# A recurrent transformer layer on one core: where local attention mixes, copies and shifts its values

## The reference, cut to what matters

```
q, k, v = split(xn @ w_qkv.T); q, k = rotary(q), rotary(k)
bq = windows(q)                      # 8 windows of 64
bk, bv = look_around(windows(k)), look_around(windows(v))   # previous window + own
attn = softmax(mask(bq @ bk.T / 8))
out = (attn @ bv) ... @ w_lo.T
```

## Time and profile before

| | us |
|---|---|
| median of 3 executions | 759.84 |
| lowest and highest | 759.74, 760.39 |
| profiled execution, its span | 759.2 |
| PE busy | 719.5 |
| DVE busy | 474.4 |
| ACT busy | 424.8 |
| POOL busy | 234.5 |

### The profile page before, as it was taken

One profiled execution on the slowest core, in us unless ns is written; L12 is line 12 of the kernel. 1 busy time (PEld: TensorE's weight loads), 2 busy tenths in 40 slices (PEclk: granted clock), 3 DMA queues, 4 the chain that ended last, 5 costly groups with the idle time before them and its releaser, 6 DMA issues.

```text
span 759.2 us, 17502 instructions
## 1 busy us (share of the span) xinstructions
PE 719.5 (95%) x6154; PEld 572.1 (75%) x6160; DVE 474.4 (62%) x1021; ACT 424.8 (56%) x1548; POOL 234.5 (31%) x364
## 2 busy tenths in 40 slices
PE   4899999999999899999999999989999999999996
PEld 3678888878887577777777778868788787877866
DVE  6433333359886787787877786574655646556575
ACT  2444444432223567677677677684756647557473
POOL 2130000000003598777766673023223131331000
PEclk9999999999999999999999999999999999999999
DMA  8701000000000323333333332000000000000001
GB/s 246 302 1 57 1 0 0 0 0 0 0 1 15 94 68 78 88 75 92 78 85 79 81 92 53 2 2 18 10 7 17 0 19 1 2 0 0 0 1 55
DMA packets 26190, 32.70 MB, mean 43 GB/s; under 512 B 7184, under 2 KB 15888, under 8 KB 25488
## 3 DMA queue, kind: packets, MB, share of 16 engines
q1 hardware_dynamic: 24848, 29.27, 14.0%
q0 software_dynamic: 1280, 2.62, 1.3%
HBM read 12.98 MB, written 2.10 MB: 20 GB/s over the span
## 4 chain that ended last, share of the span: by engine, by line
PE 55%; issue 10%; POOL 9%; DVE 8%; POOLq 7%; ACT 6%; DMA 2%; DVEq 1%; SPq 1%; ACTq 0%
PE ps L778 9%; PE ps L766 9%; PE ps L1034 7%; PE ps L1101 6%; POOLq L587 5%; PE ps L1068 4%; PE ps L1084 4%; POOL early L579 4%; PE ps L753 4%; PE ps L747 4%; PE ps L1077 2%; ACT stage L1343 2%; POOL stage L586 2%; POOLq L589 2%; POOL early L598 2%
## 5 line engine op out<-in xcount | busy, mean ns | idle before, releaser
L579 POOL TENSOR_TENSOR early<-stage 128x512 f32<-128x512 f32 x64 | 89.9, 1425 | 54.9 <-DVE stage L1708 39.7
L1343 ACT ACTIVATE stage<-ps,nmB 128x128 f32<-128x128 f32 x256 | 90.2, 381 | 27.1 <-DVE nmB L1741 26.9
L1412 ACT ACTIVATE early<-ps,nmC 128x128 f32<-128x128 f32 (+1 forms) x224 | 78.0, 370 | 30.9 <-DVE nmC L1802 30.9
L778 PE MATMUL ps<-stage 128*128 128x128 f32 (+2 forms) x448 | 86.1, 321 | 1.4 <-DVE stage L1602 1.3
L766 PE MATMUL ps<-stage,early 128*128 128x128 f32 (+2 forms) x448 | 87.1, 324 | 0.0
L766 PEld LDWEIGHTS ps<-stage,early 128*128 128x128 f32 x448 | 66.0, 194 | 24.5 <-issue 15.5
L778 PEld LDWEIGHTS ps<-stage 128*128 128x128 f32 x448 | 65.5, 191 | 12.1 <-issue 1.9
L1068 PEld LDWEIGHTS ps<-stage,early 128*128 128x128 f32 x448 | 55.5, 191 | 22.3 <-issue 22.1
L1288 ACT ACTIVATE stage<-ps 128x512 f32<-128x512 f32 x64 | 31.5, 491 | 65.2 <-PE ps L766 65.2
L1597 DVE COPY stage<-ps 128x512 f32<-128x512 f32 x32 | 22.1, 692 | 71.3 <-PE ps L753 70.9
L1799 DVE TENSOR_REDUCE nmC<-ps 128x4 f32<-128x512 f32 (+1 forms) x56 | 36.5, 652 | 46.6 <-PE ps L1068 46.6
(11 more groups left out here) (203 smaller groups left out, 1516.2 us busy)
## 6 DMA issues: line engine op xcount, KB each, us to landing
early<-early SPq DMA_DIRECT2D x256, 64.0 KB, 2.0
x<-in_x SPq DMA_DIRECT2D x4, 256.0 KB, 3.7
stage<-in_cq SPq DMA_DIRECT2D x1, 1024.0 KB, 8.1
stage<-in_ck SPq DMA_DIRECT2D x1, 1024.0 KB, 10.1
stage<-in_cv SPq DMA_DIRECT2D x1, 1024.0 KB, 12.1
stage<-in_co SPq DMA_DIRECT2D x1, 1024.0 KB, 14.1
early<-in_wqk SPq DMA_DIRECT2D x1, 1024.0 KB, 16.0
xrows<-xhat SPq DMA_DIRECT2D x1, 1024.0 KB, 5.6
```

What stands on the lines that cost most here:

```text
L579: pool.tensor_tensor(to, a, b, (ALU.subtract, ALU.add)[f]).then_inc(rot_in, 1)
L778: t = pe.matmul(ps[:, b, q0:q1], vN[:, b % 2, m, :], simA[:, b % 2, s, at:at + q1 - q0], start=False, stop=False, skip_group_check=True)
L1343: t = act.activation(pB[:, u % 2, at, :], ps[:, 4 + h, i * P:(i + 1) * P], ACT.Exp, bias=nmB[:, u % 2, at:at + 1], accum_out=rsB[:, u % 2, ...
L1412: act.activation(pC[:, k, hg, 0:n], ps[:, 5 + k, hg * P:hg * P + n], ACT.Exp, bias=nmC[:, k, hg:hg + 1], accum_out=rsC[:, k, hg:hg + 1])
```

## The change: what it does

It moves work between the rounds of three loops. DVE and SP keep theirs.

- PE, round u: **mix(u-2)**, scores(u), turn(u-1), **project(u+4)**, out(u-2), **values(u)**. Mix moves from the middle of round u+1 to directly in front of the masks and scores of round u+2; values move from the round before to the end of their own.
- ACT, round u: **mixed(u-2)**, probs(u-1), exp(u, 0), exp(u, 1), **valued(u)**.
- POOL, round u: **shifted(u-1)**, add(u+4), extra(u). Before it was shifted(u+1): the shift moves two rounds back in POOL's order. The shift of unit 0 ahead of the loop is gone, that of unit 31 stands behind it.
- The mix, its copy and the output product of unit 30 now stand in the first steps of the next stage.

```diff
 # POOL
-            shifted(0)
             add(2)
             add(3)
...
             for u in range(NU):
-                if u + 1 < NU:
-                    shifted(u + 1)
+                if u > 0:
+                    shifted(u - 1)
                 if u + 4 < NU:
                     add(u + 4)
...
+            shifted(NU - 1)
 # PE, b_values(u) and b_turn_probs(u)
-                if u >= 2:
-                    pe.wait_ge(pT_in, 2 * (u - 1))
+                if u >= 1:
+                    pe.wait_ge(pT_in, 2 * u - 1)
...
-                pe.wait_ge(vB_in, min(u + 2, NU))
+                pe.wait_ge(vB_in, u + 1)
 # PE, ahead of the loop and in it
-            b_values(0)
...
             for u in range(NU):
+                if u > 1:
+                    b_mix(u - 2)
                 b_scores(u)
                 if u > 0:
                     b_turn_probs(u - 1)
-                if u > 1:
-                    b_out(u - 2)
-                if u > 0:
-                    b_mix(u - 1)
-                if u + 1 < NU:
-                    b_values(u + 1)
                 if u + 4 < NU:
                     b_project(u + 4)
...
+                if u > 1:
+                    b_out(u - 2)
+                b_values(u)
 # PE, start of the next stage
                 if not before:
+                    b_mix(end - 1)
                     b_turn_probs(end)
-                    b_out(end - 1)
...
                 expand(g, b, it, 0)
+                if not before:
+                    b_out(end - 1)
 # ACT
-            b_valued(0)
...
             for u in range(NU):
+                if u > 1:
+                    b_mixed(u - 2)
                 if u > 0:
                     b_probs(u - 1)
                 b_exp(u, 0)
                 b_exp(u, 1)
-                if u > 0:
-                    b_mixed(u - 1)
-                if u + 1 < NU:
-                    b_valued(u + 1)
+                b_valued(u)
```

More of the change, by code:

```diff
@@ L1439, in sequence @@
                 if not before:
+                    b_mixed(end - 1)
                     b_probs(end)
```

## The result

The changed kernel takes 802.72 us (801.58 to 805.45, five runs) against 759.74 us (759.28 to 760.39): a ratio of 1.058, 95% interval 1.0561 to 1.0599, slower. The forecast was 792 with a range of 780 to 808. In the profiled execution the span went from 759.2 to 799.8 us, +40.6.

A forecast was written before the change was run, and what follows sets the result against it. PE and POOL were taken as both nearly full; the late shift closes a two-round loop, adding 32.0 us (239.4 against 207.4 to scores(29)), other edits -1.05 and +1.1, to the median 759.84: 792 us, range 780 to 808.

The forecast's parts named there:

- a loop over two rounds: Local attention: scores(v), exponentials, norm, rope, add(v+4), extra, shifted(v), mix(v), scores(v+2); 16.79 us with a gather, against 14.3 before.
- gather and shift 3.94: POOL, rounds with a gather: 0.16 to start, 0.99 gather, 0.62 first copy, 1.66 drain, 0.51 second copy; 3.94 us.
- 3.13: POOL's add when normalizing runs beside it, in us; the prediction charged 2.50 instead, saying 3.13 would make the sum 8.8 higher.
- the fallen clock: Rival: PE's granted clock falls from 2.4 to 1.2 GHz, a round is 14.1 us of PE, about 985 us; 3%.
- The sum: Local attention: scores(29) 239.4 us behind scores(0) against 207.4, +32.0; the even chain puts scores(28) 231.7 behind.
- values(0) off the path ahead: Ahead of the loop, values(0) and its copy leave the path where PE goes straight on: -1.05 us.
- The end: values(31) come to stand in round 31, ahead of mix(30) and the last turn: +1.1 us.
- The rest at nothing: Other edits, such as dropped mix waits, earlier project(u+4), turn(u) needing valued(u), and later out(30): no effect on time.
- The first: Rival: the shift stays hidden and POOL's own pace goes on binding, needing a loop of at most 14.3 us; 758.8 us, 7%.
- the drain behind each gather: POOL, between shift copies: 1.66 us charged each; a rival had it shrink to 0.13, giving 777 us, 7%.
- All contended: Rival: adds at 3.13, normalizing at 1.51 and drains at 2.4 us together, +27.7, up to 820 us; 10%.
- the forecast's own case: The two-round loop at full clock, 792 us with bounds of 786 to 806; 73%.

The follow-up runs named there:

- the extra piece out of it: Changed kernel with picks or gather ahead of add(u+4) in POOL's round, the shift staying where the change put it: 763.8 us, ratio 1.0078 to the kernel before.
- a longer copy: Changed kernel with the first copy of each shift, and its drain, made twice: 818.1, 818.5 and 821.3 us, ratio 1.0818 to the kernel before.
- Keeping PE busy: Changed kernel with matmuls of zeros in PE's waits ahead of mix in rounds 2, 4, ..., 24: 794.0 us, ratio 1.0471 to the kernel before.
- the shift in its own round: Changed kernel with POOL's round u beginning with shifted(u) instead of shifted(u-1): 759.0 us, ratio 1.0009 to the kernel before.
- the last placement of the picks: Picks four a round in rounds 1 to 3 and 24 to 28, in the kernel before and the changed kernel with shifted(u) in round u: 753.9 us each.
- the other two placements: Picks in rounds 24 to 27, or two a round over 2 to 17: kernel before 755.9, 759.6 us; changed kernel with shifted(u) in round u 759.8, 764.3.
- the shift alone: Kernel before with only POOL's move, shifted(u-1) in round u, PE and ACT as before: 976.0 us, ratio 1.2875.
- spread picks: Picks two a round over rounds 2 to 17: 759.6 us in the kernel before, 764.3 us in the changed kernel with shifted(u) in round u.

## Why the prediction was right, and where it was short

- **The mechanism** came as written: a loop over two rounds through rope, add, gather, shift and mix. It is shown in four ways: with the shift out of it the cost is gone (759.0), with the extra piece out of it nearly gone (763.8), its terms stand in the trace, and a longer copy lengthens the waits of every second mix.
- **Its terms.** 5.82 to the exponentials measured 5.82; normalizing and rope 3.22, measured 3.21; the add 2.50, measured 2.50; gather and shift 3.94, measured 3.7 (390.41 to 394.10); two rounds 16.79, measured 16.54 at full clock. From unit 5 on the add met the normalizing for 0.2 us at most, as the prediction had it: a pair of add instructions takes 2.53 us on average (1267 ns each) against 2.85 before (1425 ns), and I was right not to charge 3.13. Only the add at 261.05 had a normalizing beside it for 1.1 us; it stayed at 2.49, and the normalizing took 1.65.
- **The step that was short** is the clock. I gave the fallen clock as a rival of all or nothing, 3%, on the argument that PE would be busy for 84% of a round. But PE's wait comes as one piece, 2.5 to 6.1 us in every second round, and behind six of the first twelve pieces mix and scores run at 1.2 GHz for a while: 1.98 us for a mix of 1.15. That lengthens a two-round step from 16.5 to 17.3 and more where it happens. The first such wait and what follows it (columns as above, the granted clock third from the end):

```profile
266.00:270.00 4.00, 0.94 (x18) 0.97 (x20) 1.21 (x2) 0.00 (x0) 3.54 (x8) 0.62 0.43 102
270.00:274.00 4.00, 4.00 (x61) 3.36 (x58) 0.57 (x1) 0.60 (x1) 4.00 (x8) 0.52 0.26 62
```

  The sum had scores(28) 231.7 us behind scores(0); they stood 242.7 behind (250.72 to 493.37). 9.5 of the 11.0 lie in the steps with picks (20.2 us each, for 17.80) and with a gather (172.5 us in ten, for 167.9), the rest behind them. Keeping PE busy gave back 7.3 us of the whole, and with it scores(28) stood 233.2 us behind scores(0): at full clock the sum was right within 1.5 us, with small errors of both signs in it (2.4 us more in the steps with picks, 1.3 less in those with a gather). So this is a partial fall of the clock inside the likeliest case, a term that the sum put at nothing. The Trainium skill's "HAM oscillation" in "TensorE: Matmul & The Clock Gate" describes the pattern, waits for data that make the clock fall again and again. The trace agrees in part: the granted clock fell in some rounds and not in others, 0.96 on average from 294 to 440 us.
- **The start of the loop.** add(4) was let go at 261.05 by a placing DMA, not by rope, which had ended at 260.03: 1.0 us that I had put at nothing. The even units' picks took 4.14 and 4.02 us there, for 3.71.
- **The other edits.** values(0) off the path ahead: scores(0) came 2.1 us sooner (250.72 for 252.85), where I had 1.05. But scores(0) of the kernels that keep values(0) stood between 251.0 and 252.9 as well, so how much of it is the edit stays open. The end took 0.55 us more, for 1.1. The rest at nothing holds within the noise in two pairs (759.0 us for 758.3 with the shift in its own round, 753.9 for 753.9 with the last placement of the picks too); the other two placements leave 4 to 5 us open, as said above.
- **Mix behind the projection.** The prediction listed one loop. With PE's old order the same late shift closes a second one, of one round, and the cost is 218 us; I hadn't looked for it, and missed it again in the expectation for the shift alone. The change is free of it, since mix(u-1) stands behind project(u+4) in its order.
- **The rivals.** The first would have needed a loop under 14.3 us; it had 16.5. POOL still stands in the drain behind each gather, 22.3 us in 20 times, 1.1 us on average and 2.5 at most, for the 1.66 charged; it is not gone. All contended did not come: adds stayed at 2.50.
- **A slip in the bounds.** With -4 for the drain the lower bound of the forecast's own case would be 788, not 786. Nothing hangs on it.

## What to carry to other kernels

Before a step is moved later on one engine, write down which event the step ahead of it waits for; if that event hangs on what the moved step feeds, a loop closes, and its length divided by the rounds that it spans is the new round, if that is more than the work of a round. Add up its terms from one trace, and look at how many rounds of distance each order leaves, for every engine that the path crosses; a slack that no wait shows (here POOL's two rounds) is what such a move spends. Where the sum leaves a wait of some us in front of matmuls, set bounds with those behind it at the lower clock too. And before reordering the engine that looks busiest, level the one that the chain of waits runs over; here that gave 4.3 us, and reordering PE nothing.

## What the runs showed of the hardware

- In the changed kernel the granted clock fell to 1.2 GHz behind the waits of PE of 6.11 and 4.15 us, and behind 4 of the 10 waits of 2.47 to 2.95 us, with no order by length: it fell behind 2.60 at 359.57 and 2.55 at 410.69, but not behind 2.85 at 343.03 or 2.60 at 394.20. PE was busy for 85% of 294 to 440 us all the same.
- Behind a gather POOL's first copy begins about 1 us after the gather does (1.0 to 1.4), but the drain behind that copy is long: the second copy begins 2.8 to 4.1 us after the gather, in the kernel before and in the changed one. Without a gather the drain is 0.13 us (461.21 + 0.60 to 461.94 in the kernel before), and with an add between the gather and the shift, 0.22. Whether a gather would hold an add directly behind it no run shows.
- A pair of adds took 2.50 us alone. In the kernel before and in those with spread picks it took 2.9 to 3.5 us where it met a normalizing on DVE for 0.5 us or more from its first half on, and the normalizing then took up to 1.8 for 0.69. Three pairs whose normalizing began only in their second half stayed at 2.49 and 2.50 (261.05 in the changed kernel, 260.57 and 295.32 in the one with spread picks and the shift in its own round); the normalizing took 1.44 to 1.65.
